# A GNN and mixture-of-experts kernel: integer row numbers kept in SBUF, written-out gathers, and a GCN table of three bfloat16 parts a row

## The reference, cut to what matters

```python
# GCN: sum over incoming edges, with the square roots of both degrees
h = x @ W.T
msgs = (dinv[src] * dinv[dst])[:, None] * h[src]
out = segment_sum(msgs, dst, n) + b
# GAT: softmax over the incoming edges of each node and head
e = leaky_relu(al_src[src] + al_dst[dst], 0.2)
alpha = exp(e - emax[dst]) / (denom[dst] + 1e-16)
out = segment_sum(h[src] * alpha[:, :, None], dst, n)
```

## Time and profile before

| | |
|---|---|
| median of 3 runs | 9155.21 us |
| lowest and highest | 9154.03 and 9161.17 us |
| profiled execution, its span from first to last instruction | 9151.0 us |
| mean granted TensorE clock over the span | 0.702 |
| busy: PE, DVE, POOL, ACT | 6665, 4323, 3597, 1306 us |

### The profile page before, as it was taken

The page is one execution under the profiler, slowest core; times in us unless marked ns, Lnnn a source line. Parts: engine busy times, 40 slices in busy tenths (PEclk is TensorE's granted clock), DMA queues, the critical chain, the costliest instruction groups (busy, mean ns, idle before and its releaser), DMA issues. The chain is left out here.

```text
span 9151.0 us, 114001 instructions
## 1 busy us (share of the span) xinstructions
PE 6665.2 (73%) x27673; PEld 5205.8 (57%) x27673; DVE 4322.7 (47%) x16357; ACT 1306.3 (14%) x4560; POOL 3597.3 (39%) x3827
## 2 busy tenths in 40 slices
PE   3455555555555577776999999999999999981596
PEld 2333333333333466665777777777777777761364
DVE  8822222222222355554555555555555555556244
ACT  0000000000000133333211111111111111110121
POOL 0066666666666200000344444444444444430202
PEclk9967777677677788888755655555565666555798
DMA  2033333333333200000222222222222222220222
GB/s 78 29 91 91 91 91 91 91 92 91 91 91 92 57 0 0 0 0 24 85 65 63 64 63 64 63 64 63 64 64 64 63 65 63 63 64 17 73 74 84
DMA packets 264330, 580.90 MB, mean 63 GB/s; under 512 B 66160, under 2 KB 142768, under 8 KB 264164
## 3 DMA queue, kind: packets, MB, share of 16 engines
q0 software_dynamic: 178912, 491.51, 19.1%
q1 hardware_dynamic: 85380, 88.95, 3.0%
HBM read 532.43 MB, written 49.20 MB: 64 GB/s over the span
## 5 line engine op out<-in xcount | busy, mean ns | idle before, releaser
L1131 POOL DMA_INDIRECT gat_steps_rows<-table,gat_steps_index x1808 | 1717.2, 950 | 2234.1 <-PE gat_steps_sum_ps L1364 1612.6
L550 PE MATMUL gcn_steps_sum_ps<-gcn_steps_rows,gcn_steps_onehot 128*128 128x256 f32 x3616 | 1367.3, 544 | 1246.4 <-DMA gcn_steps_rows<-table,gcn_steps_index 869.8
L507 POOL DMA_INDIRECT gcn_steps_rows<-table,gcn_steps_index x1808 | 1719.2, 951 | 1318.2 <-ACT gcn_steps_index L491 689.9
L550 PEld LDWEIGHTS gcn_steps_sum_ps<-gcn_steps_rows,gcn_steps_onehot 128*128 128x128 f32 x3616 | 938.0, 272 | 1675.3 <-DVE gcn_steps_onehot L525 779.5
L1364 PE MATMUL gat_steps_sum_ps<-gat_steps_rows,gat_steps_onehot 128*128 128x260 f32 x3616 | 1792.5, 619 | 0.0
L533 DVE TENSOR_TENSOR acc<-gcn_steps_sum_ps,acc 128x256 f32 x452 | 192.0, 425 | 1891.7 <-PE gcn_steps_sum_ps L550 1891.7
L1364 PEld LDWEIGHTS gat_steps_sum_ps<-gat_steps_rows,gat_steps_onehot 128*128 128x128 f32 x3616 | 894.2, 287 | 92.3
L1350 PEld LDWEIGHTS gat_steps_cand_ps<-gat_steps_cand,gat_steps_onehot 128*128 128x128 f32 x3616 | 719.6, 282 | 94.1 <-DVE gat_steps_cand L1173 38.9
L1357 PEld LDWEIGHTS gat_steps_edge_ps<-gat_steps_dst_max,gat_steps_onehot_t 128*128 128x128 f32 x3616 | 710.5, 291 | 0.5 <-DVE gat_steps_dst_max L1204 0.5
L1357 PE MATMUL gat_steps_edge_ps<-gat_steps_dst_max,gat_steps_onehot_t 128*128 128x8 f32 x3616 | 663.1, 312 | 0.0
L1350 PE MATMUL gat_steps_cand_ps<-gat_steps_cand,gat_steps_onehot 128*128 128x5 f32 x3616 | 661.4, 307 | 0.7 <-DVE gat_steps_cand L1173 0.7
(11 more groups left out here) (295 smaller groups left out, 7448.3 us busy)
## 6 DMA issues: line engine op xcount, KB each, us to landing
gcn_steps_rows<-table,gcn_steps_index POOLq DMA_INDIRECT x1808, 2.7
gat_steps_rows<-table,gat_steps_index POOLq DMA_INDIRECT x1808, 2.8
expert_w<-in_L_ffn_w SPq DMA_DIRECT2D x16, 1024.0 KB, 9.6
sent<-setup_zeros SPq DMA_DIRECT2D x8, 1040.0 KB, 13.1
expert_xe<-sent SPq DMA_DIRECT2D x8, 1040.0 KB, 5.8
answers<-expert_y SPq DMA_DIRECT2D x64, 128.0 KB, 1.7
table<-gat_table_row SPq DMA_DIRECT2D x49, 130.0 KB, 1.9
x_all<-in_x SPq DMA_DIRECT2D x1, 6272.0 KB, 27.5
```

Source lines behind the costliest of these rows:

```text
L507: ins = nc.gpsimd.indirect_dma_start(out=rows[r][:, t, :], out_offset=None, in_=g["table0"][:, :], in_offset=bass.IndirectOffsetOnAxis(ap= ...
L550: ins = nc.tensor.matmul(sum_ps[r % 2][:, :], onehot[r % 2][:, t, :], rows[r][:, t, :], start=(t == 0), stop=(t == T - 1))
L1131: nc.gpsimd.indirect_dma_start(out=rows[r][:, t, :], out_offset=None, in_=g["table1"][:, :], in_offset=bass.IndirectOffsetOnAxis(ap=index[ ...
```

## The change

- `edges[0]`, the source row numbers, is an int32 tensor from setup on, and the gathers of both graph layers take their row numbers from its columns. ACT's casts, the two index buffers and their semaphores go.
- Both gather loops of POOL are written out: 1808 gathers each in a straight line, with a wait against a constant before the first gather of a step. In the GCN steps POOL no longer waits for the landing of its gathers. The raise of `slots_taken` goes.
- `table0` holds three bfloat16 parts a row, 1536 bytes: the value rounded, the rest of it rounded, and the rest of that. ACT makes the first (`high`), VectorE the other two (`split`) in the GCN table phase, two blocks behind `scale`, and SP stores them from two buffers.
- In the GCN steps the one-hots are bfloat16 and each tile has three bfloat16 matmuls, which sum the three parts into the same float32 PSUM.
- A bfloat16 iota, which setup had, is kept for the one-hots.

```diff
@@ gcn_table_phase @@
+            def store(i, k):
+                sp.wait_ge(parts_ready, i + 1)
+                sp.dma_start(g["table0"][bass.ds(i * P, P), :], parts[k][:, :, :].rearrange("p s d -> p (s d)")
+                             ).then_inc(rows_out[k], 16)
+
+            in_pairs(sp, NB, store)
+            for k in range(2):
+                sp.wait_ge(rows_out[k], 16 * ((NB + 1 - k) // 2))
...
+            def split(i, k):
+                dve.wait_ge(high_ready, i + 1)
+                ch.link(v.tensor_tensor(left[k][:, :], tile_at(g["acc"], i, D), parts[k][:, 0, :], ALU.subtract))
+                ch.link(v.tensor_copy(parts[k][:, 1, :], left[k][:, :]))
+                v.tensor_tensor(parts[k][:, 2, :], left[k][:, :], parts[k][:, 1, :], ALU.subtract).then_inc(parts_ready, 1)
...
+            with dve.Fori(1, NB // 2 - 1) as j:
+                ch.begin(j - 1, 4)
                 norm(j * 2 + 2, 0)
                 scale(j * 2, 0)
+                split(j * 2 - 2, 0)
                 norm(j * 2 + 3, 1)
                 scale(j * 2 + 1, 1)
+                split(j * 2 - 1, 1)
+            ch.end(NB // 2 - 2)
...
+            def high(i, k, first=False):
+                act.wait_ge(rows_scaled, i + 1)
+                if not first:
+                    act.wait_ge(rows_out[k], (i - k) * 8)
+                nc.scalar.copy(parts[k][:, 0, :], tile_at(g["acc"], i, D)).then_inc(high_ready, 1)
...
+            with act.Fori(2, NB // 2) as j:
+                move(j * 2, 0)
+                high(j * 2 - 2, 0)
+                move(j * 2 + 1, 1)
+                high(j * 2 - 1, 1)
@@ gcn_steps_phase @@
-        index = [sb(f"index{k}", [P, R * T], I32) for k in range(2)]
-        rows = [sb(f"rows{k}", [P, T, D]) for k in range(R)]
-        onehot = [sb(f"onehot{k}", [P, T, P]) for k in range(2)]
+        index = g["edges"][0]
+        rows = [sb(f"rows{k}", [P, T, 3 * D], BF16) for k in range(R)]
+        onehot = [sb(f"onehot{k}", [P, T, P], BF16) for k in range(2)]
         sum_ps = [ps(f"sum_ps{k}", D) for k in range(2)]
...
-            def indices(j, k):
-                act.wait_ge(index_used, j + 1)
-                nc.scalar.copy(index[k][:, :], tile_at(g["edges"][0], j, R * T)).then_inc(index_ready, 1)
-
-            in_pairs(act, TRIPS, indices)
...
-            def gather(j, k):
-                pool.wait_ge(index_ready, j + 1)
-                for r in range(R):
-
-                    pool.wait_ge(sums_ready, j * R + (r + 1))
-                    pool.sem_inc(slots_taken, 1)
-                    for t in range(T):
-                        n = r * T + t
-                        ins = nc.gpsimd.indirect_dma_start(
-                            out=rows[r][:, t, :], out_offset=None, in_=g["table0"][:, :],
-                            in_offset=bass.IndirectOffsetOnAxis(ap=index[k][:, n:n + 1], axis=0)).then_inc(rows_in[r], 16)
-
-                for r in range(R):
-                    pool.wait_ge(rows_in[r], (j + 1) * (16 * T))
-                pool.sem_inc(index_used, 1)
-
-            in_pairs(pool, TRIPS, gather)
+            for n in range(STEPS4):
+                r = n % R
+                pool.wait_ge(sums_ready, n + 1)
+                for t in range(T):
+                    nc.gpsimd.indirect_dma_start(
+                        out=rows[r][:, t, :], out_offset=None, in_=g["table0"][:, :],
+                        in_offset=bass.IndirectOffsetOnAxis(ap=index[:, n * T + t:n * T + t + 1], axis=0)
+                        ).then_inc(rows_in[r], 16)
...
-                    ins = v.tensor_scalar(onehot[r % 2][:, t, :], g["iota"][:, :],
+                    ins = v.tensor_scalar(onehot[r % 2][:, t, :], g["iota_b"][:, :],
                                           g["edges"][1][:, bass.ds(j * (R * T) + (r * T + t), 1)], None, ALU.is_equal)
...
-                    ins = nc.tensor.matmul(sum_ps[r % 2][:, :], onehot[r % 2][:, t, :], rows[r][:, t, :],
-                                           start=(t == 0), stop=(t == T - 1))
+                    for part in range(3):
+                        ins = nc.tensor.matmul(sum_ps[r % 2][:, :], onehot[r % 2][:, t, :],
+                                               rows[r][:, t, part * D:(part + 1) * D],
+                                               start=(t == 0 and part == 0), stop=(t == T - 1 and part == 2))
@@ gat_steps_phase @@
-            def gather(j, k):
-                pool.wait_ge(index_ready, j + 1)
-                for r in range(R):
-
-                    pool.wait_ge(slots_free, j * R + (r + 1))
-                    pool.sem_inc(slots_taken, 1)
-                    for t in range(T):
-                        n = r * T + t
-                        nc.gpsimd.indirect_dma_start(
-                            out=rows[r][:, t, :], out_offset=None, in_=g["table1"][:, :],
-                            in_offset=bass.IndirectOffsetOnAxis(ap=index[k][:, n:n + 1], axis=0)).then_inc(rows_in[r], 16)
-
-            in_pairs(pool, TRIPS, gather)
+            for n in range(STEPS4):
+                r = n % R
+                pool.wait_ge(slots_free, n + 1)
+                for t in range(T):
+                    nc.gpsimd.indirect_dma_start(
+                        out=rows[r][:, t, :], out_offset=None, in_=g["table1"][:, :],
+                        in_offset=bass.IndirectOffsetOnAxis(ap=index[:, n * T + t:n * T + t + 1], axis=0)
+                        ).then_inc(rows_in[r], 16)
...
-            def indices(j, k):
-
-                s.copy(index[k][:, :], tile_at(g["edges"][0], j, R * T)).then_inc(index_ready, 1)
...
-                if ahead and r == 0:
-
-                    indices(j + 1, 1 - k)
@@ program @@
-        g = {"table0": nc.dram_tensor("table0", [NB * P, D], F32).ap(),
+        g = {"table0": nc.dram_tensor("table0", [NB * P, 3 * D], BF16).ap(),
-            g["edges"] = [sb(f"edges{n}", [P, SQ * P * T], F32, graph) for n in range(4)]
+            g["edges"] = [sb(f"edges{n}", [P, SQ * P * T], F32 if n else I32, graph) for n in range(4)]
```

More of the change, by code:

```diff
@@ L143, in setup_phase @@
         dhi = sb("dhi", [P, ECOLS])
[L144 removed]
+        iota_b = g["iota_b"]
         oh_lo = [sb(f"oh_lo{k}", [P, HCH, P], BF16) for k in range(2)]
@@ L336, in gcn_table_phase @@
         xn_t = [sb(f"xn_t{k}", [P, KC, P]) for k in range(2)]
+        parts = [sb(f"parts{k}", [P, 3, D], BF16) for k in range(2)]
+        left = [sb(f"left{k}", [P, D]) for k in range(2)]
         xt_ps = [ps(f"xt_ps{k}", D).rearrange("p (c n) -> p c n", c=KC) for k in range(2)]
@@ L351, in gcn_table_phase @@
         rows_scaled = sem("rows_scaled")
-        rows_out = sem("rows_out")
+        high_ready = sem("high_ready")
+        parts_ready = sem("parts_ready")
+        rows_out = [sem(f"rows_out{k}") for k in range(2)]
         block = ctx.enter_context(nc.Block())
@@ L381, in scale @@
                                 ALU.mult).then_inc(rows_scaled, 1)
+            def split(i, k):
[3 more added lines that the diff above has]
+                v.tensor_tensor(parts[k][:, 2, :], left[k][:, :], parts[k][:, 1, :], ALU.subtract).then_inc(parts_ready, 1)
             norm(0, 0)
             norm(1, 1)
-            with dve.Fori(0, NB // 2 - 1) as j:
+            norm(2, 0)
+            scale(0, 0)
+            norm(3, 1)
+            scale(1, 1)
+            ch.end()
+            with dve.Fori(1, NB // 2 - 1) as j:
+                ch.begin(j - 1, 4)
                 norm(j * 2 + 2, 0)
                 scale(j * 2, 0)
+                split(j * 2 - 2, 0)
                 norm(j * 2 + 3, 1)
                 scale(j * 2 + 1, 1)
+                split(j * 2 - 1, 1)
+            ch.end(NB // 2 - 2)
             norm(NB - 1, 0)
             scale(NB - 3, 0)
+            split(NB - 5, 0)
             scale(NB - 2, 1)
+            split(NB - 4, 1)
             scale(NB - 1, 0)
+            split(NB - 3, 0)
+            split(NB - 2, 1)
+            split(NB - 1, 0)
         @block.scalar
@@ L1294, in weights, with step @@
                              x.rearrange("p t h -> p (t h)"), ACT.Exp).then_inc(weights_ready, 1)
-            def step(j, r, k, last, ahead):
+            def step(j, r, first, last):
                 if not last:
@@ L1310, in _ @@
             onehots(0, 0)
-            for r in range(R):
-                step(0, r, 0, False, True)
-            assert TRIPS % 2 == 1
-            with act.Fori(0, (TRIPS - 3) // 2) as m:
-                for r in range(R):
-                    step(m * 2 + 1, r, 1, False, True)
-                for r in range(R):
-                    step(m * 2 + 2, r, 0, False, True)
-            for r in range(R):
-                step(TRIPS - 2, r, 1, False, True)
-            for r in range(R):
-                step(TRIPS - 1, r, 0, r == R - 1, False)
+            run(act, step)
         @block.tensor
@@ L1914, in program @@
              "x": sb("x_all", [P, NB, D]),
-             "iota": sb("iota", [P, P]), "pidx": sb("pidx", [P, 1]), "ident": sb("ident", [P, P]),
```

(1 more changed line is left out.)

26 lines of the change are left out of this document (10 added, 16 removed).

## The result

The changed kernel took **8619.41 us** (median of 4 runs, 8598.99 to 8689.84) against 9154.62 us for the kernel before: a ratio of 0.9435, 95% interval 0.9394 to 0.9475. The forecast was 8811 us with 8700 to 8900, so the direction held and the size did not. The profiled execution took 8639.17 us of its own time, with a span of 8637.4 us, 20 us above the median.

A forecast was written before the change was run, and what follows sets the result against it. POOL's gather chain was taken to bound the GCN steps, PE (not alone) the GAT steps. 9151.0 − 320 + 52 − 75 − 1 = 8807 us of span, plus 4.2, gave 8811 us, range 8700 to 8900 (8 in 10).

The forecast's parts named there:

- Part 1: GCN gathers: removing the cast and landing wait at trip boundaries gains 320 us, bounds 300 to 339.
- nine odd pauses: GCN steps: POOL gaps of 2.06 us with no named cause, outside the boundaries; 16 us, expected to stay.
- part 2: GCN gathers: rows of 1536 instead of 1024 bytes cost nothing, as POOL's time does not depend on the row.
- Rival (e): GCN gathers: boundaries were code fetching, stalls come in their place, GCN gives nothing; 9131 us, chance 0.03.
- rival (d): GCN gathers: POOL's time per gather grows with the row's bytes, 951 to 1427 ns; 9649 us, chance 0.04.
- Part 3: GCN steps: bfloat16 products and one-hots cost nothing, covered by POOL; products of 1.7 and 3.3 us.
- Rival (c): GCN steps: PE becomes the bound because weight loads are not hidden; 9084 or some 8960 us, chance 0.09.
- Part 4: GCN table: splitting into three parts makes a block 2.2 us instead of 1.29; cost 52 us, bounds 38 to 95.
- Part 5: GAT gathers: a wait directly before the gather saves 0.45 us in 166 steps; gain 75 us, bounds 0 to 198.
- rival (b): GAT steps: all of PE's waits there vanish and the clock gains by it; 8688 us, chance 0.06.
- Part 6: Starts of both gather stages: first gathers come some 0.5 us earlier, gain 1 us; edges tensor and iota cost nothing.

The follow-up runs named there:

- landing experiment: Changed kernel with POOL's wait for all landings put back after every 16 gathers of the GCN steps; 8945.89 us, ratio 0.9786.
- GAT-only: Kernel before with only the GAT part of the change, GCN table and GCN steps as before; 8982.73 us, ratio 0.9791.
- float32 kernel: Changed kernel with float32 table, rows, one-hots and products back in the GCN layer; 8754.06 us, in another hour 8542.03 us.
- first four experiments: Changed kernel with, one at a time: semaphore raise put back, raise before the wait, ACT's casts back, landing wait back; 8836.5, 8586.53, 8586.19, 8945.89 us.
- raise back: Changed kernel with POOL's semaphore raise put back between the wait and the first gather of each GAT step; 8836.5 us, ratio 0.9668.
- raise first: Changed kernel with the semaphore raise put in front of POOL's wait in the GAT steps; 8586.53 us, ratio 0.9416.
- freed by tile: Changed kernel with GAT row buffers freed tile by tile, POOL waiting before each gather for its tile; 8295.74 us, ratio 0.9085.
- both: Changed kernel with float32 table, rows and products in GCN and GAT row buffers freed tile by tile; 8259.34 us, again 8322.88 us.

## Why the prediction was right or wrong, point by point

**Part 1, boundaries: right in the mechanism, 2 us beyond its bound.** −341 for −320 (bounds −300 to −339). Waiting for landing was the cause and the cast a small rest, as the landing experiment shows. The nine odd pauses, which I had kept at 16 us, went too, so POOL's gaps fell by 333 us where I had 323; the rest is mostly the gathers' own time, part 2. Rival (e), that the boundary was code fetching, did not come; the changed kernel's gathers run on in 1807 gaps of which none is above 0.31 us. By that, what I took from the Trainium skill, Runtime: NRT & Kernel Launch, Instruction fetch mechanics, agrees with this trace. The nine pauses of the landing experiment stand in straight code too; what they come from no run here shows.

**Part 2, longer rows: right.** 946 ns a gather against 951, so rival (d) fell; over 1808 gathers that is a gain of 9 us that the sum does not have. DMA share 0.56 where I had forecast 0.53; landing 3.1 us, where it was 2.7.

**Part 3, products and one-hots: right to cost nothing, too dear in the pieces.** 1.47 and 2.73 us a product at the two clocks, where I had 1.7 and 3.3. The matmuls start 0.109 and 0.213 us apart, where I had 0.128 and 0.256 us a pair: at half clock twelve of 256 columns last 12 × 0.213 = 2.56 us, and PE needs 0.17 more, so the weight loads (94 to 153 ns, 677 us in all) lie beside the matmuls. Rival (c) fell. The 107 ns that I took from the Trainium skill, TensorE: Matmul & The Clock Gate, section LDWEIGHTS, lie within the range measured, but they do not add to the round.

**Part 4, the table: +36 for +52, just under the bound of +38.** The split is as priced, 1.21 us from 431.14 to 432.35. But a block takes 1.99 us and not 2.2: norm and scale start 0.33 us apart although norm lasts 0.41, and the next norm starts before the split has ended, so VectorE overlaps the end of one operation with the next, which I had kept for the bound. 49 × (1.99 − 1.29) is 34 us, so the tail that I had at 7 cost only some 2.

**Part 5, GAT: this is the step that failed.** It had the right cause (the raise, a separate increment between wait and gather) and priced it at 0.45 us × 166 steps = −75; measured were −212, beyond its bound of −198. Two errors. The gap shortened by 0.54 us, not 0.45, and PE's waits by 112 us in all. And I let the term end with the waiting: PE's busy time fell by 109 us as well, the same instructions at a higher granted clock. I cut the stage into its 451 steps to see where (the table is in the last section). PE waits for rows almost only in steps that had the upper level for a part: 210 of them before, 235 after. These went from 7.69 to 6.90 us, 0.79 each or 166 us; the 25 that changed sides gave another 2.1 us each, 52 us. Steps at the lower level take 8.99 us after 8.96, no less than before. So PE does wait in about as many steps as I had counted, but the gain lies in all of those partly at the upper level and is 0.79 us in each, not 0.45 in 166.

That is near rival (b)'s mechanism, with half of its premise. I gave it 0.06 and 123 us, since "the clock gains" had no price in it beyond the waits. My bounds left no room either: all taken at their low ends (−339, +38, −198, −1) they give 8655 us, and 8619 lies below.

What is shown: in all four profiles with the raise behind the wait these steps take 7.69 to 7.72 us, and in all ten with the wait on the gather and buffers freed by the step 6.84 to 7.02. What is not shown is what sets how many steps get the upper level: with the raise behind the wait it was 210 to 217 of 451, without it 235 to 258 in five profiles, 121 and 167 in the GAT-only and the float32 kernel, and 396 to 431 in another hour. The small waits of those two kernels are no sign of a better path: the waits come with the steps partly at the upper level, of which they had few. Whether fewer waits raise the clock is therefore argued at most.

**Part 6 and the rest: right**, within 1 and 3 us. With −212 in the place of −75, and +36 for +52, the prediction's sum would have been 9151 − 320 + 36 − 212 − 1 = 8654 us of span, 17 above the 8637 measured; the GCN steps gave 21 more, some 4 went elsewhere.

## What to carry to other kernels

Put a wait on the instruction that it is meant to release: a cheap semaphore instruction between them made each release 0.54 us later, and here the stage some 210 us longer. Free buffers in the pieces in which they are refilled. And where PE is the bound at a clock below its upper level, price a shorter wait by PE's busy time as well, with a range that admits as much again; then measure often, since the runs of one kernel spread over 91 us (changed) to 348 us (float32 table) here.

## What the runs showed that I had not expected

**One kernel, two ways to 8620 us.** In a later hour, on two chips, the changed kernel had GCN steps of 2600 us and GAT steps of 3252 and 3164, with medians of 8623 and 8638 us. Timeline of its second profile in the GCN steps:

```profile
1503.56 2.74 PE L576 MATMUL gcn_steps_sum_ps<-gcn_steps_rows,gcn_steps_onehot 128*128 128x256 bf16 x12 [1.60 <-issue]
1504.35 0.94 POOL L537 DMA_INDIRECT gcn_steps_rows<-table,edges  x1 [0.30 <-issue]
...
1506.85 0.95 POOL L537 DMA_INDIRECT gcn_steps_rows<-table,edges  x1 [0.30 <-issue]
1510.17 0.42 DVE L558 TENSOR_TENSOR acc<-gcn_steps_sum_ps,acc 128x256 f32 x1 [6.66 <-remote]
1510.29 0.94 POOL L537 DMA_INDIRECT gcn_steps_rows<-table,edges  x1 [2.50 <-remote]
```

The product ends at 1506.30, and the addition that waits for nothing else starts at 1510.17, 3.9 us later, where it was 0.14 in the first profile (1504.98 to 1505.12). It was over 1 us late in 170 of 452 steps. POOL starts its next gather 0.12 us behind that addition, and waited like this 149 times, some 2.5 us each. I then ran the kernel before and the changed one together:

> The unedited kernel before, for its profile in the same hour as the next one. Theory A (what held the written-out gathers up in the last profile of the changed kernel is a condition of the chip in that hour): if it is still there, products' ends reach DVE several us late here too, and the GCN steps last 2640 to 2700 us; if it is gone, 2610 +- 10. Theory B (it belongs to written-out gathers that never pause): the end of a product reaches DVE within 0.2 us throughout, whatever the next one shows.

> The changed kernel a third time. In its second profile the GCN steps took 2600 us and the GAT steps 3252, where the first had 2269 and 3583, with the same sum. If the first split comes back (2269 and 3500 to 3600, mean clock of the runs 0.67 to 0.70), the second was a condition of that hour; if the second comes back (2600 and 3250, clock 0.71 to 0.73), both are states of this kernel, and its median of 8620 holds in either.

```profile
495.00:3096.00 2601.00, 1103.49 (x5424) 679.86 (x5424) 542.01 (x2259) 0.00 (x0) 1714.65 (x1808) 0.63 0.49 137
4438.00:7602.00 3164.00, 3050.24 (x14464) 2217.24 (x14464) 2297.96 (x10395) 630.22 (x2712) 1723.30 (x1808) 0.73 0.29 76
```

The late ends are in the kernel before too (121 of 452), so they are not the change's doing; it pays only 9 us for them in its GCN steps, perhaps because its pauses at the boundaries let PE catch up. Its runs without a profile were longer as well, 9177 and 9180 us against 9136 to 9155 in the other hours. The 2640 to 2700 us that I had expected for its GCN steps did not come. Between these two profiles the GCN part of the change is worth 18 us and its GAT part 641, in the first ones 341 and 212; the changed kernel's was the fastest of its four executions, though, 87 us under their median. Three further runs were to tell what each part hangs on in that condition:

> The raise between wait and gather back in the GAT steps, once more. If the whole GAT gain comes from the earlier release in every condition, GAT takes 3797 +- 10 us here as in the first run of this edit; with GCN steps of 2600 the kernel is then at 9160 to 9180, no faster than before, and with GCN steps of 2270 at 8836 again. If something else made GAT 3164 to 3252 us long in the second and third profile of the changed kernel, GAT stays below 3400.

> The wait for all landings at the end of each trip back in the GCN steps, once more. If the ends of products are punctual in this hour, 2586 us again. If they are late: theory A (a pause lets PE and VectorE catch up, as in the kernel before) gives 2590 to 2620, so no loss against the written-out gathers without a pause; theory B (lateness and pauses add) gives over 2750.

All ends were punctual, and the numbers are those of the first time (3788 and 2585 us). These runs were on neither of the two chips that had shown the late ends, so they tell nothing of that condition; one of the two had run the first four experiments without it, so it is not the chip alone. It stays open what delays the ends, why GAT gains so much at the same time, and whether the equal totals are more than chance. The traces with late ends also hold only about half of the semaphore events of the others (44,685 against 85,930 for the changed kernel), so that their releasers ("remote") say little.

**Two kinds of steps in GAT.** In GAT no kernel had the upper level for more than 0.47 of the stage, though PE was busy for 94 to 99% of it. The table counts the 451 steps from one first transpose of a row buffer's scores to the next (L1332 in the changed kernel, L1331 before): those whose mean granted clock was over 0.52, so that a part of them ran at the upper level, and the others. The wait is PE's for the rows.

| kernel | partly at the upper level | mean us | wait in each, us | at the lower level | mean us |
|---|---|---|---|---|---|
| before | 210 | 7.69 | 0.94 | 241 | 8.96 |
| raise back | 215 | 7.72 | 0.95 | 236 | 8.96 |
| raise back, again | 217 | 7.70 | 0.94 | 234 | 8.96 |
| unchanged, later hour | 215 | 7.72 | 0.96 | 236 | 8.99 |
| changed | 235 | 6.90 | 0.37 | 216 | 8.99 |
| raise first | 258 | 6.84 | 0.37 | 193 | 8.98 |
| GAT only | 121 | 7.02 | 0.45 | 330 | 9.01 |
| float32 table | 167 | 6.90 | 0.39 | 284 | 9.01 |
| changed, third | 431 | 6.86 | 0.12 | 20 | 9.14 |
| freed by tile | 255 | 6.42 | 0.00 | 196 | 8.97 |
| both | 354 | 6.65 | 0.00 | 97 | 8.94 |

The edit decides how long a step partly at the upper level is, and hardly how long one at the lower level is. How many there are differs between kernels with the same GAT code, and between hours for one kernel; what decides that stays open. The float32 kernel of the first measurement fell, about a third into the stage, into steps of 7.0, 9.1, 8.99 and 8.99 us over and over, at the upper level for 0.10 of the time, and stayed there; the same kernel in another hour had 431 steps of 6.84 us and a share of 0.47. Its runs lay between 8488.85 and 8873.52 us over both. Medians of kernels that differ in GAT's clock alone are to be read with that spread in mind.
